# The second layer's heads: squares moved from ScalarE to GpSimd, and the last five tiles cut into groups of three and two

## The reference, cut to what matters

```python
x = x + _L1_gnn_ref(_layernorm(x), L1_gnn_W, L1_gnn_a, src, dst)

h = einsum('ni,hio->nho', x, W)               # 3125 x 8 x 32
hs, hd = h[src], h[dst]
diff = hd - hs
lin = hs.a1 + hd.a2 + diff.a3 + abs(diff).a4 + (hs*hd).a5     # one number per edge and head
alpha = where(lin > 0, lin, 0.2*lin)          # then a softmax over the edges of a source
```

## Time and profile before

| | us |
|---|---|
| median of 3 runs | 2702.91 |
| lowest, highest | 2701.94, 2704.18 |
| the profiled execution's own time | 2699.96 |
| its span | 2698.2 |
| the stage `heads` in it, first bring to first instruction of `scores` | 1390.17 to 1448.27 |

### The profile page before, as it was taken

How to read it: one execution, slowest core, us unless ns; L and a number is a source line. 1 busy time by engine, 2 the same in 40 slices (tenths; PEclk the granted TensorE clock), 3 DMA queues, 4 the chain that set the end, 5 groups by cost and what they waited for, 6 DMA issues and landing times. The chain is left out here.

```text
span 2698.2 us, 60536 instructions
## 1 busy us (share of the span) xinstructions
PE 2131.9 (79%) x15054; PEld 1745.1 (65%) x15055; DVE 1638.1 (61%) x4143; ACT 1457.7 (54%) x3571; POOL 1382.9 (51%) x1373
## 2 busy tenths in 40 slices
PE   4789966676767599999936888888884989679990
PEld 3666634444444499999925777788783777469990
DVE  8889963333333733333267777877777878853337
ACT  6779943333332443343347666666665888333335
POOL 0000067777777133333224777777762999236650
PEclk9889986766666699999967999999896999889995
DMA  3210036433333501111135887887772888552224
GB/s 114 95 58 21 22 92 198 136 105 105 105 105 100 200 33 35 37 36 36 41 109 155 236 237 237 241 239 236 231 218 98 269 268 246 185 188 70 70 66 146
DMA packets 181373, 365.89 MB, mean 136 GB/s; under 512 B 30042, under 2 KB 67332, under 8 KB 180974
## 3 DMA queue, kind: packets, MB, share of 16 engines
q1 hardware_dynamic: 118489, 208.65, 22.7%
q0 software_dynamic: 52608, 145.53, 19.6%
q10 hardware_dynamic: 10133, 9.97, 1.1%
HBM read 272.20 MB, written 91.83 MB: 135 GB/s over the span
## 5 line engine op out<-in xcount | busy, mean ns | idle before, releaser
L904 POOL DMA_INDIRECT weightsL_w<-y_gnn,all_slot_dst x416 | 397.7, 956 | 283.8 <-POOLq L84 157.3
L833 POOL DMA_INDIRECT scores_rows<-h_gnn,all_slot_dst x440 | 431.7, 981 | 157.3 <-issue 133.5
L963 PE MATMUL sum_ps<-weightsL_w 128*128 x880 | 348.8, 549 | 153.5 <-SPq L889 91.6
L963 PEld LDWEIGHTS sum_ps<-weightsL_w 128*128 128x128 f32 x880 | 221.0, 271 | 281.7 <-issue 247.3
L977 DVE TENSOR_TENSOR sums_acc<-sums_acc,sum_ps 128x256 f32 x440 | 185.3, 421 | 317.4 <-PE sum_ps L963 267.9
L1654 ACT ACTIVATE sums_acc<-expertsL_hid_ps,expertsL_b 128x128 f32<-128x128 f32 x704 | 198.2, 373 | 300.9 <-PE expertsL_hid_ps L1603 300.6
L1603 PE MATMUL expertsL_hid_ps<-sums_acc,expertsL_w 128*128 128x128 f32 x2816 | 337.3, 277 | 5.0 <-DVE sums_acc L1674 3.0
L2145 PE MATMUL scores_diff_ps<-all_ident,scores_rows 128*128 128x128 f32 x880 | 294.7, 335 | 55.6 <-DMA scores_rows<-h_gnn,all_slot_dst 45.9
L1603 PEld LDWEIGHTS expertsL_hid_ps<-sums_acc,expertsL_w 128*128 128x128 f32 x2816 | 327.1, 193 | 5.6 <-issue 5.5
L1615 PE MATMUL expertsL_out_ps<-weightsL_w,sums_acc 128*128 x1408 | 323.6, 379 | 0.0
L1578 POOL DMA_INDIRECT ys_L<-sums_acc,ffnL_result x120 | 130.0, 1083 | 348.3 <-DVE sums_acc L1684 321.4
(11 more groups left out here) (456 smaller groups left out, 4193.0 us busy)
## 6 DMA issues: line engine op xcount, KB each, us to landing
saved_gnn<-scores_rows SPq DMA_DIRECT2D x220, 264.0 KB
sum_rows<-saved_gnn SPq DMA_DIRECT2D x220, 264.0 KB, 3.2
weightsL_w<-in_L_ffn_W SPq DMA_DIRECT2D x16, 1024.0 KB, 9.1
weightsL_w<-in_L_ffn_w SPq DMA_DIRECT2D x32, 512.0 KB, 9.8
scores_lanes<-slot_lanes SPq DMA_DIRECT2D x44, 320.0 KB, 5.2
sort_low_b<-low_lanes SPq DMA_DIRECT2D x32, 416.0 KB, 3.5
weightsL_w<-ys_L SPq DMA_DIRECT2D x6, 1280.0 KB, 11.9
scores_rows<-h_gnn,all_slot_dst POOLq DMA_INDIRECT x440, 5.1
```

Of the source, the lines that this page charges most:

```text
L833: pool.indirect_dma_start(out=self.rows[:, s, :], out_offset=None, in_=table[:, :], in_offset=bass.IndirectOffsetOnAxis(ap=e["slot_dst"][: ...
L904: pool.indirect_dma_start(out=rows[:, at:at + D], out_offset=None, in_=table[:, :], in_offset=bass.IndirectOffsetOnAxis(ap=e["slot_dst"][: ...
L963: last = nc.tensor.matmul(ps[(PAIRS * turn + s // 2) % len(ps)][:, s % 2 * D:(s % 2 + 1) * D], pick[h][:, s % HALF, :], rows[:, bass.ds(pl ...
```

## The change

The squares are computed by POOL with a `tensor_tensor` multiply of the rows with themselves. In POOL's list `square_of(n)` stands behind a bring: that of tile 8 for group 0, 12 for group 1, 18 for group 2, 22 for group 3; the last two groups' squares stand behind the bring of tile 24. ACT's list loses its five squares. The groups are now of 5, 5, 5, 5, 3 and 2 tiles, so DVE has six rounds instead of five, and SP six stores. The casts of the last two groups stand at the end of ACT's list.

```diff
+    SIZES = (G, G, G, G, 3, 2)
-        groups = [slice(g, g + G) for g in range(0, NT, G)]
+        groups = [slice(sum(SIZES[:n]), sum(SIZES[:n + 1])) for n in range(len(SIZES))]
 @block.gpsimd
+                def square_of(n):
+                    pool.wait_ge(kept, groups[n].stop)
+                    if n:
+                        pool.wait_ge(weighed, n)
+                    mine = row[:, groups[n], 0:D]
+                    nc.gpsimd.tensor_tensor(work[:, 0, 0:SIZES[n], :], mine, mine, ALU.mult).then_inc(squared, 1)
+
+                behind = 0
                 for t in range(0, NT, 2):
                     if t >= RING:
                         pool.wait_ge(turn_done, t - RING + 1)
                     nc.gpsimd.tensor_scalar(staged[:, t % RING, :], x[:, t, :], ...).then_inc(brought[0], 1)
+                    if t >= groups[behind].stop + 2:
+                        square_of(behind)
+                        behind += 1
+                for n in range(behind, len(groups)):
+                    square_of(n)
 @block.scalar
-                def square_of(n):
-                    act.wait_ge(kept, groups[n].stop)
-                    if n:
-                        act.wait_ge(weighed, n)
-                    nc.scalar.activation(work[:, 0, :, :], row[:, groups[n], 0:D], ACT.Square).then_inc(squared, 1)
...
-                    if n >= 0 and k == 0:
-                        square_of(n)
...
-                square_of(len(groups) - 1)
-                for part in (1, 2):
-                    round_off(len(groups) - 1, part)
+                for n in range(NT // G - 1, len(groups)):
+                    for part in (1, 2):
+                        round_off(n, part)
```

More of the change, by code:

```diff
@@ L1920, in heads @@
     RING = 4
-    w, half, norm = h["w"], h["ends"][:, 2, :].unsqueeze(1).to_broadcast([P, G, D]), h["norm"]
+    w, norm = h["w"], h["norm"]
+    SIZES = (G, G, G, G, 3, 2)
     with Names(nc, "heads") as m:
@@ L1934, in heads, with half @@
         rounded, left, squared, weighed, row_ready, stored = (m.sem(n) for n in ("rounded", "left", "squared", "weighed", "row_ready", "stored"))
-        groups = [slice(g, g + G) for g in range(0, NT, G)]
+        groups = [slice(sum(SIZES[:n]), sum(SIZES[:n + 1])) for n in range(len(SIZES))]
+        def half(n):
+            return h["ends"][:, 2, :].unsqueeze(1).to_broadcast([P, SIZES[n], D])
         with nc.Block() as block:
@@ L1969, in keep @@
                     nc.scalar.activation(row[:, t, :], out_ps[t % 2][:, 0:WIDTH], ACT.Copy).then_inc(kept, 1)
-                def square_of(n):
-                    act.wait_ge(kept, groups[n].stop)
-                    if n:
-                        act.wait_ge(weighed, n)
-                    nc.scalar.activation(work[:, 0, :, :], row[:, groups[n], 0:D], ACT.Square).then_inc(squared, 1)
                 def round_off(n, part):
                     act.wait_ge(left, 2 * n + part)
-                    nc.scalar.activation(split[:, groups[n], part, 0:D], rest[:, part - 1, :, :], ACT.Copy).then_inc(rounded, 1)
+                    nc.scalar.activation(split[:, groups[n], part, 0:D], rest[:, part - 1, 0:SIZES[n], :], ACT.Copy).then_inc(rounded, 1)
                 bring(1)
@@ L2034, in _ @@
                         ve.wait_ge(rounded, 2 * n - 1)
-                    nc.vector.tensor_tensor(rest[:, 0, :, :], mine, split[:, tiles, 0, 0:D], ALU.subtract).then_inc(left, 1)
+                    nc.vector.tensor_tensor(rest[:, 0, 0:SIZES[n], :], mine, split[:, tiles, 0, 0:D], ALU.subtract).then_inc(left, 1)
                     ve.wait_ge(squared, n + 1)
-                    nc.vector.tensor_tensor(work[:, 1, :, :], work[:, 0, :, :], half, ALU.mult).then_inc(weighed, 1)
+                    nc.vector.tensor_tensor(work[:, 1, 0:SIZES[n], :], work[:, 0, 0:SIZES[n], :], half(n), ALU.mult).then_inc(weighed, 1)
                     ve.drain()
                     ve.wait_ge(rounded, 2 * n + 1)
-                    nc.vector.tensor_tensor(rest[:, 1, :, :], rest[:, 0, :, :], split[:, tiles, 1, 0:D], ALU.subtract).then_inc(left, 1)
-                    nc.vector.tensor_reduce(square[:, tiles, :], work[:, 1, :, :].rearrange("p t (h d) -> p t h d", d=HD), AX, ALU.add)
+                    nc.vector.tensor_tensor(rest[:, 1, 0:SIZES[n], :], rest[:, 0, 0:SIZES[n], :], split[:, tiles, 1, 0:D], ALU.subtract).then_inc(left, 1)
+                    nc.vector.tensor_reduce(square[:, tiles, :], work[:, 1, 0:SIZES[n], :].rearrange("p t (h d) -> p t h d", d=HD), AX, ALU.add)
                     ve.drain()
```

## The result

The changed kernel takes 2690.99 us, median of 20 runs, against 2703.11 us for the kernel before, also 20 runs. The ratio is 0.9952 with a 95% interval of 0.9933 to 0.9970: 12 us less, where 2.6 us more was predicted, with a range of 2699.6 to 2709.3 us. A single pair of profiles can't tell where 12 us go; the means over all profiles further down can.

A forecast was written before the change was run, and what follows sets the result against it. ACT's list was taken to pace DVE until 1433 us, then DVE itself. Last addition +3.1 (0.9 rounds, 0.95 extra round, 1.2 races), end -0.5: +2.6 on 2702.91 gives 2705.5 us; 8 in 10 within 2699.6 to 2709.3.

The forecast's parts named there:

- terms for group 0: First group: cast 0.95, square 2.4 and first remainder 1.5 us in a row, so nothing gained at DVE's second remainder.
- the races in the tail: Last two groups: POOL's square first holds DVE 1.5 and 1.0 us, DVE first costs nothing; half counted, +1.2 us.
- the end: From DVE's last addition to `scores`: the smaller last store lands 1.1 us sooner, DVE's path ends the stage, 0.5 gained.
- a change outside the stage: Listed sign that the prediction is wrong; what follows `heads` was expected only to move.
- The port: Squares on POOL exclude DVE's two-input or two-port-mode instructions for their whole length; DVE's addition comes 1.16 us late per round.
- The rounds: DVE's second remainders 8.88 us apart against 8.58 now; three rounds put that of group 3 0.9 later.
- the 0.5 us for the brings: In each round, brings behind POOL's square delay DVE's cast by 0.3 and its first remainder by 0.2 us.
- The square's price: One five-tile square on POOL takes 2.5 us, with bounds of 2.34 and 2.9.
- The tail: DVE's work from group 3's second remainder to its last addition: one round more costs 0.95 us, the races 1.2.
- Rival A: The port doesn't matter or squares fall where DVE idles: -2.7 us, 2700.2 us; chance 0.26.
- Rival B: A square costs 2.9 us or more on POOL and late brings stall PE: 2708.9 us; chance 0.20.
- Rival C: Both sides cancel because DVE takes the port first at every contested point: 2702.9 us; counted within the main case's 0.54.

The follow-up runs named there:

- tt_first: Kernel before (plus a PE maximum with 0), with six one-element GpSimd multiplies without waits ahead of the brings of `heads`: 2701.84 us, ratio 1.0009.
- tt_one: Kernel before (plus a PE maximum with 0), with a single one-element GpSimd multiply behind the brings of `heads`: 2687.25 us, ratio 0.9957.
- tiny: Kernel before (plus a PE maximum with 0), with six waits and six one-element GpSimd multiplies behind the brings: 2689.36 us, ratio 0.9947.
- act_split: Changed kernel (plus a PE maximum with 0) with squares back on ScalarE, groups of three and two kept: ratio 0.9997 to the kernel before, slow chip.
- again_scalar: Changed kernel (plus a PE maximum with 0), with six one-element tensor_scalar operations on GpSimd behind its last square: 2696.57 us, ratio 0.9995.
- pool_five: Changed kernel (plus a PE maximum with 0) with five groups of five, squares still on GpSimd: ratio 1.0016 to the kernel before, slow chip.
- memset_wait: Kernel before (plus a PE maximum with 0), with six waits and six one-element GpSimd memsets behind the brings: 2702.37 us, ratio 0.9996.
- tiny_nowait: Kernel before (plus a PE maximum with 0), with six one-element GpSimd multiplies without waits behind the brings: 2688.22 us, ratio 0.9953.

## Why the prediction was wrong, by its own steps

**The step that failed** is the sentence that what follows `heads` starts behind a barrier and should only move, with the silence on what stands before it. The rest of the kernel is 12 us shorter. What the runs showed in its place: GpSimd's gathers there take 0.946 instead of 0.953 and 0.957 us as soon as a multiply or a copy, of one element even, stands behind the brings in GpSimd's list of `heads`. The gather stages are paced by these instructions, so 856 of them carry the difference (12.6 us of busy time between tt_first and tt_one). Neither ScalarE's relief nor the group sizes are needed for it (tiny, tt_one), nor does the group split produce it (act_split). Inside the stage 2.6 us more was forecast and 0.56 less came: a second failure, of the terms for group 0, the races in the tail and the end below. None of my rivals had the first; "a change outside the stage" stood only in the list of what would prove me wrong.

**The port** was right. POOL and DVE exclude each other in the squares as in the earlier trace rows, down to 2.16 us for an addition of 40 elements. So says the Trainium skill, SBUF — State Buffer, section Who interferes with whom, of a two-input instruction of VectorE beside a reading one of GpSimd. By that rule, the trace agrees; and the sum L2050, a reduction, for which that section of the Trainium skill excludes a conflict, keeps its 1.47 us at 1424.71 beside the square of 1425.04.

**The rounds** were right in kind and 0.4 us too dear in all: L2049 comes after 9.15, 8.96 and 8.14 us, 26.25 in sum against 25.73 before and 26.6 predicted. That the sum is so near is in part luck. Counted from ACT's cast R, square 1 was to start at R + 3.2; it started at R + 4.3 (1403.63 to 1407.93), since the keep in front of it came a us later, and the next one at R + 4.1 (1412.78 to 1416.89), since POOL was still in the three brings that end there. Only the third kept to R + 3.3 (1421.74 to 1425.04). On the other side the 0.5 us for the brings was nothing: behind each square DVE's cast kept its 0.95 and L2044 its 1.49, and the brings waited instead (the three at 1410.24 last 6.68 us, against 3.66 for the first three of the stage). And the square was 0.2 shorter. Third round: 8.88 - 0.5 - 0.2 = 8.2, measured 8.14. ACT's freed time became waiting in one of the three rounds (the 1.02 us at 1421.74).

**The square's price** of 2.5 us was too high: 2.32, just under the lower bound of 2.34 from the earlier trace rows. (The upper bound of 2.9 left out the fixed 0.19 us; with it, 1280 times a quarter above 1.83 ns is 3.1.) The scaling from 256 elements of one partition was the wrong row; the one of the same shape was nearer. The estimate of 2.8 to 2.9 us from the Trainium skill, GPSIMD Engine Reference, section 3.1, is not met.

**Group 0** was mis-sized by 0.9: I put L2040 at the same distance from the stage's start, 17.38 us; it came at 16.44. Cast, square and first remainder took 4.2 us in a row, not 4.9, and the remainder was ready just when ACT came to its cast. L2049 started 1.46 us behind that cast, not 1.58 (L2037 and its drain end 1.41 + 1.57 - 1.54 = 1.44 behind `left`, so 1.58 was a slip). From DVE's first cast to L2049, where nothing scatters, it is 5.72 us instead of 6.53: 0.8 of the 0.94 are the change's, the rest is where the stage began.

**The tail** cost 11.01 - 10.06 = 0.95 us, exactly the extra round. The half counted for the races, 1.2 us, was not there: DVE was first both times, by 0.06 us at group 3.

**The end** gave 1.09 us (3.84 from the last addition to `scores`, 4.93 before), not 0.5. Of this 0.38 is DVE's own: its small instructions behind the addition end after 2.63 us instead of 3.01, because an idle 0.43 us in front of one cast is gone, here and in act_split. I had taken the 1.39 us of the border before `heads` for the way from DVE's end to `scores`; it is 1.2 here (1444.98 to 1446.19), and 0.9 in act_split and again_scalar, which nothing explains. That DVE's path now ends the stage fits: the last store lands 2.2 us after its issue, at 1444.8. Before, the last store took 3.7, the longest of the earlier trace rows, not the 3.4 that I used.

Sum for the stage: -0.94 + 0.52 + 0.95 - 1.09 = -0.56 us, measured -0.56. Of this 0.12 is the scatter of the first cast, and 0.23 that `before` had an end of 4.93 instead of the usual 4.7; what is left is the 0.2 of the other executions. Rival A (2700.2 us) had the sign but not the reason: the port did hold. Rival B is out by the 2.32 us. Rival C, nothing gained or lost, is nearest for the stage, with half of its reason: DVE came first in the tail, POOL in the rounds.

## What to carry to other kernels

A stage paced by many equal instructions turns 10 ns of each into microseconds, so compare the median of its commonest instructions before and after, also where nothing was changed, and also ahead of the change. When a gain is larger than the changed stage can give, put the cheapest piece of the change alone into the old kernel: one multiply of one element did here what the whole change did (ratio 0.9957 against 0.9952 and 0.9960). And of two operations that contend for a port, ask which one another wait will start first; here the squares gained 0.8 us in group 0 and, alone, gave 1.6 back where they held the port; only with the shorter last groups did the stage come out ahead, by 0.2.

## What the runs showed of the hardware that was not expected

The time of GpSimd's indirect DMA instructions of the two gather stages had two levels for the same text, the same on all chips with 2700 us and within 3 to 4 ns on the one with 3044. High, 953 ns in the first aggregation and 957 in `scores`: as it was, with memsets (6 or 10) behind the brings, with multiplies ahead of the brings or in the first stage, with plain copies in place of ScalarE's squares. Low, 946 and 946 (947 once): with 1, 6 or 10 multiplies or 6 copies of one element behind the brings, or with the squares there. pool_five had 949 and 949 on the slow chip. The gathers of the first mixture of experts (932 to 1313 us) went along, with medians of 1568 ns in the high group and 1560 to 1562 in the low one; again_scalar had 1566. The 64 gathers of the second mixture (972 to 974 ns) and the indirect DMAs that write `ys_L` in both mixtures (987) didn't.

What stays open is why. The first aggregation runs before the instruction that changes it, in the same execution; so either something is kept from one execution to the next, or it depends on how the program lies in memory, which two pairs speak against but don't exclude: memset against multiply, equal in number (memset_wait and tiny), and tt_first against tiny_nowait, the same six multiplies ahead of or behind the brings, so that GpSimd's list is as long as the other and differs in the order inside `heads` alone. The kind of the last computation before the gathers of `scores`, memsets not counted, fits every kernel but again_scalar, where the two gather stages part (953 and 946). That six tensor_scalar operations of one element don't undo in `scores` what the squares did is not explained.
